# Heads' results scaled and split in PSUM, with every step of the plan given a new due time

## The chip, the cores and the metric

The kernel runs on one core of a Trainium2 chip. The metric is the device time of one execution in microseconds; smaller is better. TensorE (PE), VectorE (DVE), ScalarE (ACT) and GpSimd (POOL) each have an instruction stream of their own and meet through semaphores. SyncE (SP) issues all transfers.

## What is computed

Two blocks stand one after the other on x of shape (8, 1024, 512), in float32. The first is cross-attention with 8 heads of width 64; the second is self-attention with 16 heads of width 32, normalised queries, a gate over the heads' results, and a projection.

```python
def attn(q, k, v):                       # per head
    return softmax(q @ k.T * scale) @ v
# block X ("not ffn"), per batch
q = layernorm(x) @ Wq; k, v = ctx @ Wk, ctx @ Wv
x = x + tanh(g_xattn) * (heads(attn(q, k, v)) @ Wo + bo)
# block F ("ffn"), per batch
y = layernorm(x)
q, k, v = y @ Wq.T + bq, y @ Wk.T + bk, y @ Wv.T + bv
q = (q / norm(q) + query_embedding) * softplus(temperature)
h = heads(attn(q, k, v))
gates = softmax(h @ Wr.T + br); routed = top 3 of them; sw = softmax(h @ Ws.T + bs)
x = x + tanh(g_ffn) * ((h * sum of masked gates) @ Wp.T + bp)
```

## The kernel before

**Precision.** Every projection is made in three passes: a float32 operand is split into a rounded part ("hi", ScalarE, type fp32r) and the rest ("lo", VectorE, source minus hi), and hi·hi, hi·lo and lo·hi are summed in PSUM.

**Work and stages.** There are 16 batches of work: j = 0 to 7 are block X, j = 8 to 15 are block F. A batch has four groups g of 128 channels (2 heads of 64 in X, 4 heads of 32 in F), a group has two halves of 512 queries, and a half (number h, 8 in a batch) has 8 steps T of 128 keys. One step T is:

- `S` (PE, L1039): scores of 128 keys by 512 queries for each head e, on the whole array, into a PSUM bank;
- `ex` (ACT, L1237): the exponential, PSUM to SBUF (`probs`, `more`, `added`, `added_f`: a ring of 7 buffers in X, 10 in F);
- `ad` (POOL, L926): adds the exponentials of most steps to the half's running sum;
- `PV` (PE, L1053): probabilities times values, each head in its own columns of the array, summed over the 8 steps in one PSUM bank, called `acc`.

**The end of a half** is what the change rewrites. `sm` (PE, L1065) sums the exponentials, `sma` (ACT, L1244, L1245) takes the reciprocal into `rn`, `ev` (DVE, L1408, L1409, L1414) refines it and writes `h_raw = acc * rn` to SBUF, which empties `acc` and the bank of `sm`. Then `hs` (ACT, L1250) rounds `h_raw` to `h_hi`, in block F `gt` (PE, L1073) multiplies `h_raw` with the gates' weights, `hsl` (DVE, L1401) subtracts `h_hi` from `h_raw` in place, with both operands in SBUF, and `hw` (SP, L807) stores both parts. At the end of a batch `ol` (SP, L816) loads them back, `op` (PE) projects them, `ope` (DVE, L1465) adds to x, and `st` stores.

**Other work beside the steps**, which the text calls filler: `tr` (PE, L967) turns the normalised x, `pq`, `pk`, `vp` and `op` (PE, L947) are the projections, `mx` (PE, L1021, in row tiles) and `mxr` (DVE, L1378) find the scores' maxima, four PSUM banks at a time.

**The order.** All engines run one order that a planner (`Plan.run`) makes before compilation. It walks through time with a table of durations (`TAKES`). When an engine is free it takes, of the items whose predecessors are done, the one with the lowest due time, `step`, counted in steps T. The due time is the base in the code plus a per-kind offset from `AT[...]["off"]`. So due times decide between items that are ready and never make an engine wait. Items that write PSUM also need an empty bank of the eight; a bank is free once its taker is done. PE has one more term, quoted here: while PE is in a tiled mode (`PV`, `sm`, `mx`), untiled items are put back by `held` steps, and the other way round.

```python
wanted = lambda x: (step[x] + stage(batch(x)).AT["held"] * (name == "pe" and (x[0] in self.TILED) != (tiled is not None)), str(x))
...
elif it[0] in self.SHARED:
    begin = max(now, free["pool"])
```

The second quote is how the planner reckons with `hsl` and POOL: it delays `hsl` by what is left of POOL's present instruction.

## Time and profile before

| | us |
|---|---|
| median of 3 runs | 4856.84 |
| lowest, highest | 4849.66, 4885.29 |
| the profiled execution | 4888.63 |
| its span, first to last instruction | 4886.8 |
| PE busy | 4506.7 (92%) |
| POOL busy | 3385.7 (69%) |
| DVE busy | 3069.3 (63%) |
| ACT busy | 2523.6 (52%) |
| chain that ended last: share of PE | 76% |

All times in the profile are of one execution, which lies 32 us above the median of the timed ones. A matmul's end is modelled and consecutive matmuls overlap, so the cost of a matmul is read as the distance between starts, not as its duration. A number in square brackets at the end of a row of the timeline is the idle time just before it and what ended it.

### The profile page before, as it was taken

The numbers are of one execution on the slowest core, as the hardware profiler recorded it, in microseconds if no ns is written. First come the engines' busy times: TensorE is split into PE (matmuls) and PEld (weight loads), VectorE is DVE, ScalarE is ACT, GpSimd is POOL, SyncE is SP. The second block draws the span as 40 slices with busy tenths as digits, with TensorE's granted clock in tenths as the row PEclk, the third lists the DMA queues.
The fourth block names the chain that finished last, engine by engine and source line by source line (L and its number), as shares of the span: only waits on it lengthen the run. The fifth ranks groups of instructions, "written<-read, shape, count | busy, mean of one in ns | idle before, by whom it ended". The sixth has DMA issues, their size and how long they took to land.

```text
span 4886.8 us, 67578 instructions
## 1 busy us (share of the span) xinstructions
PE 4506.7 (92%) x21568; PEld 2325.8 (48%) x21568; DVE 3069.3 (63%) x3955; ACT 2523.6 (52%) x4577; POOL 3385.7 (69%) x2667
## 2 busy tenths in 40 slices
PE   4699999999999999999899899999998999989985
PEld 3355554555555555555354454544444544435432
DVE  4464646464646464676776767676767767676774
ACT  3253535353535353546556565656556556656562
POOL 1365666676757575667778778687877787877885
PEclk8899999999999999999999999999999999999997
DMA  6456656666666566545344344353534443543522
GB/s 221 111 160 177 177 168 179 179 180 186 160 175 166 159 169 164 157 138 151 91 127 134 83 132 134 89 154 104 139 100 118 130 134 84 145 121 89 154 70 78
DMA packets 516173, 682.50 MB, mean 140 GB/s; under 512 B 42608, under 2 KB 371824, under 8 KB 506608
## 3 DMA queue, kind: packets, MB, share of 16 engines
q1 hardware_dynamic: 515824, 678.18, 49.9%
q8 instruction: 178, 2.92, 0.3%
q14 instruction: 171, 1.40, 0.1%
HBM read 323.83 MB, written 150.99 MB: 97 GB/s over the span
## 4 chain that ended last, share of the span: by engine, by line
PE 76%; issue 7%; DVE 6%; ACT 4%; DMA 3%; POOL 1%; SPq 1%; ACTq 0%; POOLq 0%; DVEq 0%
PE aux L947 26%; PE aux L1039 19%; PE aux L1053 17%; PE aux L1021 7%; PE aux L1065 3%; DVE nm L1378 3%; ACT probs L1237 2%; DVE h_raw L1401 2%; SPq L836 1%; PE aux L991 1%; PE aux L1073 1%; POOL added_f L926 1%; PE aux L967 1%; ACT more L1237 1%; DMA raw<-in_ctxT 1%
## 5 line engine op out<-in xcount | busy, mean ns | idle before, releaser
L926 POOL TENSOR_TENSOR added<-added,probs 128x512 f32<-128x512 f32 x1433 | 1823.6, 1305 | 751.2 <-PE aux L1053 496.7
L1378 DVE TENSOR_REDUCE nm<-aux 128x2 f32<-128x1024 f32 x1536 | 1808.8, 1220 | 842.2 <-PE aux L1021 841.1
L1237 ACT ACTIVATE probs<-aux 128x512 f32<-128x512 f32 x2151 | 1190.9, 597 | 1141.8 <-PE aux L1039 1092.3
L1039 PE MATMUL aux<-stack 128*128 128x512 f32 x4096 | 1409.6, 437 | 103.8 <-ACT probs L1237 50.3
L1039 PEld LDWEIGHTS aux<-stack 128*128 128x128 f32 x4096 | 707.3, 191 | 950.0 <-issue 324.5
L1053 PE MATMUL aux<-probs,v 128*32 128x512 f32 (+1 forms) x4302 | 983.9, 628 | 0.0
L926 POOL TENSOR_TENSOR added_f<-added_f,probs 128x512 f32<-128x512 f32 x537 | 677.4, 1293 | 194.7 <-PE aux L1053 180.6
L947 PE MATMUL aux<-xT_hi,wqk 128*128 128x512 f32 x1536 | 562.0, 415 | 13.5 <-DVE mrow L1393 4.6
L1021 PE MATMUL aux<-ck_hi,cq_hi 32*128 32x512 f32 (+1 forms) x3072 | 460.1, 491 | 112.6 <-DVE nm L1378 90.8
L1021 PEld LDWEIGHTS aux<-ck_hi,cq_hi 32*128 32x128 f32 (+1 forms) x3072 | 182.1, 188 | 549.6 <-issue 529.5
L947 PE MATMUL aux<-wvo,parts 128*128 128x512 f32 x1536 | 409.0, 403 | 35.0 <-issue 35.0
L1237 ACT ACTIVATE more<-aux 128x512 f32<-128x512 f32 x537 | 300.6, 598 | 208.6 <-PE aux L1039 196.8
L947 PEld LDWEIGHTS aux<-xT_hi,wqk 128*128 128x128 f32 x1536 | 289.8, 189 | 136.6 <-issue 76.3
L947 PEld LDWEIGHTS aux<-wvo,parts 128*128 128x128 f32 x1536 | 279.7, 189 | 141.7 <-issue 87.3
L926 POOL TENSOR_TENSOR added_f<-added_f,more 128x512 f32<-128x512 f32 x231 | 295.0, 1301 | 46.1 <-PE aux L1053 42.8
L926 POOL TENSOR_TENSOR added<-added,more 128x512 f32<-128x512 f32 x231 | 293.3, 1295 | 36.1 <-ACT more L1237 21.7
L947 PE MATMUL aux<-xT_lo,wqk 128*128 128x512 f32 x768 | 301.9, 393 | 0.0
L1053 PE MATMUL aux<-more,v 128*32 128x512 f32 x1074 | 300.3, 634 | 0.2 <-ACT probs L1237 0.2
L1401 DVE TENSOR_TENSOR h_raw<-h_raw,h_hi 128x512 fp32r<-128x512 f32 x128 | 290.4, 2269 | 12.0 <-ACT h_hi L1250 12.0
L1053 PEld LDWEIGHTS aux<-probs,v 128*32 128x32 f32 (+1 forms) x4302 | 158.1, 120 | 277.0 <-issue 207.8
L914 POOL TENSOR_TENSOR cq_lo<-qb,cq_hi 128x512 fp32r<-128x512 f32 x64 | 82.7, 1292 | 200.9 <-ACT cq_hi L1196 200.9
L1237 ACT ACTIVATE added<-aux 128x512 f32<-128x512 f32 x256 | 140.6, 598 | 142.1 <-PE aux L1039 142.0
(129 smaller groups left out, 4355.6 us busy)
## 6 DMA issues: line engine op xcount, KB each, us to landing
wqk<-w_split SPq DMA_DIRECT2D x256, 256.0 KB, 3.7
wvo<-w_split SPq DMA_DIRECT2D x64, 1024.0 KB, 7.3
parts<-h_kept SPq DMA_DIRECT2D x128, 512.0 KB, 4.0
stack<-cq_hi SPq DMA_DIRECT2D x128, 256.0 KB, 5.7
stack<-ck_hi SPq DMA_DIRECT2D x128, 256.0 KB, 6.0
v_kept<-v_out SPq DMA_DIRECT2D x128, 256.0 KB, 2.7
v<-v_kept SPq DMA_DIRECT2D x64, 512.0 KB, 5.3
h_kept<-h_hi SPq DMA_DIRECT2D x128, 256.0 KB, 2.4
```

Of the source, the lines that this page charges most:

```text
L836: sp.dma_start(stack[row:row + D, g % 2, e * ph.SLOTS + slot, :].bitcast(F32), src[what][half][e * D:(e + 1) * D, :].bitcast(F32)).then_in ...
L914: pool.tensor_tensor(cq["lo"][:, q], qb[:, n], cq["hi"][:, q].bitcast(F32), ALU.subtract).then_inc(qlo_ok, 1)
L926: pool.tensor_tensor(onto, onto, exp_buffer(T, e), ALU.add).then_inc(added_ok, 1)
L947: ins = pe.matmul(out, lhs(a, k), rhs(c, k), start=k == 0 and i == 0, stop=k == whole - 1 and i == 2)
L967: ins = pe.transpose(out[:, i * P:(i + 1) * P], xs[:, i, k * P:(k + 1) * P], ident[:])
L1021: ins = pe.matmul(aux[:, b, :], cq["hi"][r, t * P:(t + 1) * P], ck["hi"][r, half * HALF:(half + 1) * HALF], start=True, stop=True)
L1039: ins = pe.matmul(out, stack[:, g % 2, e * ph.SLOTS + ks, jt * P:(jt + 1) * P], stack[:, g % 2, e * ph.SLOTS + qs, n * HALF:(n + 1) * HALF ...
L1053: ins = pe.matmul(out[e * D:(e + 1) * D, :], v[:, T // STEPS % 2, jt, e * D:(e + 1) * D], exp_buffer(T, e), start=jt == 0, stop=jt == TT - 1)
L1065: ins = pe.matmul(out[e * D:(e + 1) * D, :], ones[:, 0:ph.SUM], exp_buffer(T, e), start=i == 0, stop=i == ph.APART)
L1237: act.activation(exp_buffer(T, e), aux[:, o.bank["S", T, e], :], ACT.Exp, scale=ph.SCALE).then_inc(probs_ok, 1)
L1378: dve.tensor_reduce(nm[:, half, first:first + 2 * TT - t:TT], aux[:, b:b + 2, :], axis=AX.X, op=ALU.max, negate=True).then_inc(emptied["dv ...
L1401: dve.tensor_tensor(h_raw[:].bitcast(F32R), h_raw[:], h_hi[:].bitcast(F32), ALU.subtract).then_inc(h_lo_ok, 1)
```

## The change

In the diff `h_raw_ok` replaces `h_lo_ok`, and `h_lo` takes the place of the broadcast `bv` in SBUF.

1. `ev`'s last instruction multiplies `acc` by `rn` in PSUM, in place, and no longer waits for the store of the half before.
2. `hs` reads `acc` from PSUM. In F it adds the bias of the values, one number per channel.
3. New in F: `hr` (ACT) writes `h_raw` from `acc` plus bias, for `gt` alone. `gt` waits for it.
4. `hsl` reads `acc` from PSUM and `h_hi` from SBUF, and writes `h_lo` (F) or `h_raw` (X). It no longer waits for `gt`. The bank of `acc` is free only after `hsl`.
5. The bias of the values moves out of `vpe`: that becomes a plain copy.
6. `held` is 2.3 in X and 0.08 in F (it was 0), and nearly every kind of item gets a new offset.

```diff
-AT = (dict(p=[2.5, 15.14, 35.81, 48.12], over=7.63, held=0, mx0=-7.37, mxn=12.3, ctx=[18.4, 40.15, 13.68], load=[19.73, 48.58], norm=[28.97, 50.99], turned=[27.96, 23.9], vp=[38.13, 3], out=[1.5, 1.69], xr=-21.46, split=38.75, off={"ad": -0.59, "ln": 0.31, "pka": -0.33, "pkl": -1.14, "s2": 5.61, "gt": -1.09, "sma": -2.26, "trl": 2.36, "l2": 0.99, "mx": 0.07, "tra": 0.09, "mxr": -0.9}),
-      dict(p=[0.69, 18.6, 36, 50], over=6.09, held=0, mx0=-5.5, mxn=12.04, load=[51.51, 62.62], norm=[43.61, 30.7], turned=[30.5, 37.03], vp=[39, 3], out=[-1.13, 3.73], xr=-13.34, off={"trl": -0.94, "ad": -2.39, "tra": 1.65, "l2": 2.38, "cp": -4.87, "hsl": 0.44, "ev": -0.54, "ln": -0.9, "hs": -1.11, "sma": -1.35, "pqa": 1.36, "pkl": 0.75, "s3": 0.52, "pka": -0.28, "ssa": -0.53}))
+AT = (dict(p=[8.18, 7.74, 23.19, 56.95], over=13.88, held=2.3, mx0=-12.67, mxn=6.38, ctx=[9.31, 31.84, 65.87], load=[-19.58, 32.91], norm=[66.14, 26.24], turned=[17.66, 9.47], vp=[12.54, 5.88], out=[-4.13, 3.16], xr=-50.9, split=-100.42, off={"ad": 1.99, "ln": 5.75, "pka": -2.81, "pkl": 0.78, "s2": 5.61, "gt": -1.09, "sma": 8.55, "trl": 6.57, "l2": -7.13, "mx": -12.48, "tra": -4.24, "mxr": -2.4, "PV": 1.9, "S": 0.65, "ca": -11.36, "cd": -3.32, "ce": 8.23, "ci": -14.19, "cl": -2.55, "co": -2.71, "cx": 4.69, "cxl": -4.19, "cz": -2.4, "ev": 12.87, "ex": -11.45, "fb": -3.9, "fh": -12.84, "fi": 2.38, "fl": 2.62, "fr": 0.46, "fs": 3.83, "hs": 2.31, "hsl": -1.3, "hw": -1.65, "la": -14.63, "lb": 8.21, "mc": -5.82, "md": -26.04, "ml": -4.01, "mt": -3.87, "ol": 16.37, "op": -1.15, "ope": -1.02, "pk": -11.66, "pq": 1.59, "pqa": -4.8, "pql": 4.74, "sd": -1.5, "sm": 1.94, "st": 10.15, "tr": -9.24, "vl": 0.04, "vp": -10.27, "vpe": 3.66, "vs": 7.51, "wh": 7.3, "wl": 8.21, "wlo": -10.25, "wo": 3.99, "wr": -6.16, "ws": 9.98, "wv": 10.08, "xb": 2.46, "xl": -2.44, "xq": 6.09, "xr": 5.7}),
+      dict(p=[3.21, 20.36, 38.43, 52.49], over=5.98, held=0.08, mx0=-6.04, mxn=12.62, load=[100.75, -3.84], norm=[62.84, -8.24], turned=[-10.21, 12.16], vp=[40.89, 2.6], out=[5.06, 3.2], xr=-78.15, off={"trl": 0.44, "ad": -7.13, "tra": -1.33, "l2": 33.19, "cp": -4.87, "hsl": 3.98, "ev": 2.54, "ln": -11.36, "hs": 12.75, "sma": 10.04, "pqa": -2.45, "pkl": -8.4, "s3": -16.15, "pka": -11.02, "ssa": -16.48, "PV": -0.1, "S": -0.12, "ex": 0.85, "ga": -1.82, "ge": 5.92, "gm": -2.43, "gs": -1.15, "gt": -10.64, "hr": 7.79, "hw": -0.24, "la": 4.17, "lb": -6.25, "mc": 11.04, "md": 2.98, "ml": 28.19, "mt": -6.39, "mx": 1.12, "mxr": -5.35, "ol": -21.23, "op": 1.68, "ope": -17.26, "pk": 1.3, "pq": -1.15, "s2": 6.23, "s3p": -3.33, "sd": 2.14, "sm": -3.43, "ss": 0.5, "st": 1.37, "tr": -0.23, "vl": 0.77, "vp": -3.17, "vpe": -9.01, "vs": -0.29, "wl": 6.9, "wo": 0.81, "wv": -2.39, "xb": -1.89, "xl": 14.38, "xq": 1.37, "xr": -7.51}))
...
-                self.add(("ev", h), "dve", b + 0.6, [("sma", h), ("PV", T), ("ev", h - 1), ("hw", h - 1)])
+                self.add(("ev", h), "dve", b + 0.6, [("sma", h), ("PV", T), ("ev", h - 1)])
                 if ph.ffn:
-                    self.add(("gt", h), "pe", b + 1, [("ev", h), ("fb", 0)])
+                    self.add(("hr", h), "act", b + 0.9, [("ev", h), ("gt", h - 1)])
+                    self.add(("gt", h), "pe", b + 1, [("hr", h), ("fb", 0)])
...
-                self.add(("hs", h), "act", b + 1, [("ev", h)])
-                self.add(("hsl", h), "dve", b + 1.2, [("hs", h), ("gt", h)])
+                self.add(("hs", h), "act", b + 1, [("ev", h), ("hr", h), ("hw", h - 1)])
+                self.add(("hsl", h), "dve", b + 1.2, [("hs", h)])
...
-    SHARED = ("hsl", "fl")
+    SHARED = ("fl",)
...
-                        act.activation(h_hi[:], h_raw[:], ACT.Copy).then_inc(h_hi_ok, 1)
+                            act.activation(h_raw[:], src, ACT.Identity, bias=bias).then_inc(h_raw_ok, 1)
+                            continue
...
+                        if ffn:
+                            act.activation(h_hi[:], src, ACT.Identity, bias=bias).then_inc(h_hi_ok, 1)
+                        else:
+                            act.activation(h_hi[:], src, ACT.Copy).then_inc(h_hi_ok, 1)
...
-                        dve.tensor_tensor(v_out[:], src, bv[:], ALU.add).then_inc(emptied["dve"], 1)
+                        dve.tensor_copy(v_out[:], src).then_inc(emptied["dve"], 1)
...
                         dve.wait_ge(h_hi_ok, h + 1)
+                        whole = aux[:, o.bank["acc", h], :]
                         if ffn:
-
-                            wait_full(dve, ("gt", h))
-                        dve.tensor_tensor(h_raw[:].bitcast(F32R), h_raw[:], h_hi[:].bitcast(F32), ALU.subtract).then_inc(h_lo_ok, 1)
+                            ins = dve.scalar_tensor_tensor(h_lo[:], whole, bv[:, h // 2 % NG:h // 2 % NG + 1], h_hi[:].bitcast(F32), ALU.add, ALU.subtract)
+                        else:
+                            ins = dve.tensor_tensor(h_raw[:].bitcast(F32R), whole, h_hi[:].bitcast(F32), ALU.subtract)
+                        ins.then_inc(emptied["dve"], 1)
...
-                        dve.tensor_tensor(h_raw[:], aux[:, o.bank["acc", h], :], rn[:], ALU.mult).then_inc(emptied["dve"], 1)
+                        whole = aux[:, o.bank["acc", h], :]
+                        dve.tensor_tensor(whole, whole, rn[:], ALU.mult).then_inc(emptied["dve"], 1)
```

## Rows read from the trace of the kernel before

**Rows 1.** The page's busy times, share of the span, and instructions.

```profile
PE 4506.7 (92%) x21568; PEld 2325.8 (48%) x21568; DVE 3069.3 (63%) x3955; ACT 2523.6 (52%) x4577; POOL 3385.7 (69%) x2667
```

**Rows 2.** Windows (us; busy of PE, PEld, DVE, ACT, POOL; PEclk; DMA): one batch of X, one of F.

```profile
1165.00:1414.00 249.00, 248.45 (x1044) 132.28 (x1044) 132.83 (x178) 112.02 (x202) 160.22 (x123) 1.00 0.62 167
...
3621.00:3959.00 338.00, 311.18 (x1652) 156.26 (x1648) 242.98 (x313) 200.64 (x368) 261.11 (x208) 0.96 0.42 119
```

**Rows 3.** Timeline of PE (start, duration, what) in block X.

```profile
1302.49 1.20 PE L1039 MATMUL aux<-stack 128*128 128x512 f32 x4
1303.62 1.08 PE L1053 MATMUL aux<-probs,v 128*64 128x512 f32 x4
1304.63 0.28 PE L1027 MATMUL aux<-ident,least 128*16 128x128 f32 x1
...
1307.34 0.62 PE L947 MATMUL aux<-wvo,kv_hi 128*128 128x512 f32 x2
1307.80 0.39 PE L947 MATMUL aux<-wvo,kv_lo 128*128 128x512 f32 x1
```

**Rows 4.** Chain of work that ended last (start, length): two tiled runs in block F.

```profile
4700.67 0.99 PE aux L1053 x8
4701.67 1.72 PE aux L1065 x16
```

**Rows 5.** `hsl` before: ns min/median/max, first and last start; then busy us, mean ns.

```profile
L1401 DVE TENSOR_TENSOR h_raw<-h_raw,h_hi x128: 671/1185/35294, 183.8 to 4858.9; 128x512 fp32r<-128x512 f32 x128
...
L1401 DVE TENSOR_TENSOR h_raw<-h_raw,h_hi 128x512 fp32r<-128x512 f32 x128 | 290.4, 2269 | 12.0 <-ACT h_hi L1250 12.0
```

**Rows 6.** The same view of DVE instructions that read one operand from PSUM.

```profile
L1344 DVE TENSOR_TENSOR xT_lo<-aux,xT_hi x128: 669/681/694, 26.4 to 4421.6; 128x512 fp32r<-128x512 f32 x128
...
L1353 DVE SCALAR_TENSOR_TENSOR ck_lo<-aux,bk,ck_hi x64: 740/744/752, 2069.1 to 4672.7; 128x512 fp32r<-128x512 f32 x64
```

**Rows 7.** Timeline around one long `hsl`: DVE, PE, POOL.

```profile
2946.10 7.61 DVE L1401 TENSOR_TENSOR h_raw<-h_raw,h_hi 128x512 fp32r<-128x512 f32 x1
...
2955.11 0.78 PE L1021 MATMUL aux<-ck_hi,cq_hi 32*128 32x512 f32 x4 [4.45 <-DVE nm L1378]
...
2945.68 7.48 POOL L926 TENSOR_TENSOR added<-added,probs 128x512 f32<-128x512 f32 x6
```

**Rows 8.** The waits of PE in block F, 2250 to 4740 us (total, times, longest).

```profile
PE aux L1021 <- DVE nm L1378: 64.0, 23, 8.5
PE aux L1039 <- ACT probs L1237: 37.9, 103, 1.5
PE aux L1039 <- ACT more L1237: 19.5, 58, 1.5
PE aux L1039 <- DVE nm L1378: 18.1, 13, 9.3
```

**Rows 9.** Window just after the stall of rows 7 (columns as in rows 2).

```profile
2955.00:2960.00 5.00, 4.75 (x21) 1.95 (x22) 4.29 (x5) 1.57 (x3) 2.46 (x2) 0.66 0.79 225
```

**Rows 10.** The end: timeline of DVE and POOL, a window, and the chain.

```profile
4738.09 35.29 DVE L1401 TENSOR_TENSOR h_raw<-h_raw,h_hi 128x512 fp32r<-128x512 f32 x1
...
4806.73 25.12 DVE L1401 TENSOR_TENSOR h_raw<-h_raw,h_hi 128x512 fp32r<-128x512 f32 x1
...
4825.16 1.25 POOL L926 TENSOR_TENSOR added_f<-added_f,more 128x512 f32<-128x512 f32 x1
...
4760.00:4780.00 20.00, 7.31 (x42) 3.68 (x39) 15.90 (x6) 4.34 (x9) 12.83 (x11) 0.78 0.09 27
...
4815.46 22.88 issue
...
4851.43 1.90 PE aux L1065 x16
```

**Rows 11.** Start of block X: an idle time of PE.

```profile
196.81 1.22 PE L1021 MATMUL aux<-ck_hi,cq_hi 64*128 64x512 f32 x4 [9.31 <-DVE nm L1378]
```

**Rows 12.** Duration of ACT's read of a bank with a bias, as in rows 5.

```profile
L1162 ACT ACTIVATE ck_hi<-aux,bk x64: 668/672/712, 2065.9 to 4670.3; 128x512 fp32r<-128x512 f32 x64
```

## What I predicted, and why

> **What bounds the kernel now.** I read the page's busy times first, then windows by batch, then the timeline of PE, then the waits of PE, and last the chain at the end.
>
> PE is busy for 92% of the span, POOL for 69% [rows 1]. By batch the two blocks differ [rows 2]: a batch of X takes 249 us with PE busy throughout, a batch of F 338 us with PE idle for 27 us of it and a granted clock of 0.96. So X can be faster only if the same matmuls need less PE time. F can gain from its idle time too, and both blocks from their order.
>
> In X the time between starts shows what a matmul costs [rows 3]. Two passes of a projection take 0.46 us, 0.23 each. Four passes of `S` take 1.13 us, from 1302.49 to 1303.62, where four times 0.23 are 0.91: changing into the tiled mode and back costs 0.22. The four matmuls of a `PV` take 1.01 us. Where two tiled groups of the same mode follow each other, the second is cheaper: in F one `PV` takes 0.99 us, but the 16 matmuls of `sm` 1.72, that is 0.86 a group [rows 4]. So a `PV` that follows a `PV` saves 0.22 + 0.15 = 0.37 us. In the timeline of X from 150 to 2150 us there are 549 runs of column-tiled work with four matmuls, like that of [rows 3], and 13 longer ones. Nearly every `PV` pays in full.
>
> In F the waits of PE name `mxr`, the reduction of maxima on DVE, for 82 us, and the exponentials for another 57 [rows 8]. But `mxr` isn't slow: it is late, because `hsl` stood ahead of it on DVE. An `hsl` takes 671 ns at best, 1185 in the median and 35294 at worst [rows 5], 2269 in the mean, 290.4 us for all 128. The timeline shows what stretches it [rows 7]: one begins at 2946.10 and ends when POOL's unbroken run of six adds, begun at 2945.68, ends at 2953.16. PE idles 4.45 us for the maxima behind it. It does not happen to instructions that read one operand from PSUM: 128 and 64 of them, with POOL busy through much of their time, stay within 669 to 694 and 740 to 752 ns [rows 6].
>
> The Trainium skill, "SBUF — State Buffer", section "Who interferes with whom", states that a DVE instruction with two inputs in SBUF and a GpSimd instruction that reads SBUF exclude each other for the length of one instruction, and that one with at most one SBUF input doesn't contend. By that, an `hsl` would wait for one add at most, some 1.25 us, and the long stalls would not exist: the sum below would shrink to its terms for order. The trace agrees on who contends and disagrees on how long: 7.6 us are six adds [rows 7].
>
> **The change part by part.** The sum is made against the profiled span of 4886.8 us.
>
> *`hsl` reads PSUM.* Its nearest rows are those of [rows 6]: 0.68 us in X, 0.74 in F, always. DVE loses 290 - 64 x 0.68 - 64 x 0.74 = 199 us. What of it counts is where PE waited:
>
> - In F, 2250 to 4740 us, 13 idle times of PE lie behind an `hsl` of 7.6 to 11.9 us; that of [rows 7] is typical, they run from 1.3 to 9.3 us, together 65.6 of the 82 us of [rows 8]. All go: -65.6.
> - After such a stall the granted clock is 0.66 for 5 us though PE is busy again [rows 9]: 1.7 us lost each, 13 times: -22.
> - At the start of X the first `hsl`, begun at 183.8 us [rows 5], is followed by 9.3 us of idle PE, again for the maxima [rows 11]: -9.3. Later in X PE is busy throughout [rows 2], so nothing more is to be had from `hsl` there.
> - At the end two `hsl` take 35.3 and 25.1 us [rows 10]. The second holds back the store of half 62's result, hence the projection, and PE stands 22.9 us from 4815.5. The last sum `sm` begins at 4851.4. POOL sets the limit here: it worked without a pause except for 7.2 us in the window 4760 to 4780, and its last add ends at 4826.4. Without the stalls that would be 4819, and some 5 us of PE work fall between it and `sm`: 4824 in place of 4851, -27.
>
> *`ev` multiplies in PSUM, and doesn't wait for the store; `vpe` is a copy.* Same lengths (0.69 us) within a few hundredths. 0.
>
> *`hr` is new on ACT.* 64 instructions of 0.67 us [rows 12] are 43 us more on an engine that is busy 201 of 338 us in a batch of F. Behind each stand exponentials, for which `S` and PE wait. These waits are 57 us [rows 8] in some seven batches with 1400 us of ACT work [rows 2]; in proportion 43 us add 1.7. `gt` comes 0.7 us later, and nothing on PE waits for it but its bank. Bounds: 0, if always hidden, and 43, if each delays PE in full. I take +5.
>
> *`acc` keeps its bank until `hsl`.* Before, it was free after the multiplication; now ACT's copy or copies and `hsl` follow: 0.6 + 0.7 us in X, 2.1 in F if nothing else is in front. The due times put `hs` in F 12.75 steps back, so exponentials that are ready go first. The next half uses another bank, so what is missing is one bank of eight for `S` and filler. I charge nothing while it is a few us of the 40 of a half; a rival takes the rest.
>
> *`held` = 2.3 in X.* With `S` 0.65 and `PV` 1.9 later, the due times now put `S` about three steps ahead of `PV`, where the ring of 7 buffers ends, against two before; with `held` PE stays in a mode until the other side is over two steps overdue. So `PV` should come in pairs where the exponentials are ready. Of 560 runs in all of X, if half of the `PV` pair up, 140 changes go: 140 x 0.37 = -52. Bounds: 0 (pairing fails for lack of banks or exponentials) and 280 x 0.37 = -104 (all pair up).
>
> *All other due times.* In F the bases of projections and maxima stay near their old values and `held` is 0.08, so I expect the same pattern with the small waits for exponentials partly evened out. Besides `hsl`, F idles for 7 x 27 - 65.6 = 123 us [rows 2]. I take -15, an eighth of it, between -50 (two fifths evened out) and +30 (a quarter more of it). In the first 150 us x is now due before the weights, and one stall of the size of [rows 11] may come or go there, about 10 us either way. 0. Transfers are moved on SP's queue too (`xl`, `xr`, `ol`, the splitting of F's weights), past the stores of `hw`, `vs` and `st`. No transfer is among the waits of [rows 8], and in X PE doesn't wait at all [rows 2], so they have slack, and I give them no price.
>
> Sum: 4886.8 - 65.6 - 22 - 9.3 - 27 + 5 - 52 - 15 = 4700.9; with 1.8 us outside the span, 4703. The profiled execution is 32 us above the median of before. I don't carry that over: the long stalls depend on how DVE and POOL meet, so they may be what differs between executions, and the changed kernel wouldn't have them. If it is something else, 4671.
>
> **The rivals.**
>
> *A. The forecast*, 4703. Chance 0.48.
>
> *B. Stalls go, order gives nothing.* X is at 249 us a batch in any order if `PV` can't pair. Without the 52 and the 15: 4770. For it: `mx` takes four banks at a time and `acc` now holds its own longer, so that few are left to run `S` ahead. Chance 0.22.
>
> *C. The order gives all it can.* -104 in X and -50 in F: 4616. For it: F still idles 17 us a batch besides `hsl`. Against it: each exponential must still come before its `PV`. Chance 0.12.
>
> *D. Fillers in bunches.* In X `pk`, `vp`, `tr` and `mx` get due times some ten steps earlier, so they run as soon as they are ready, and stretches without filler follow. There POOL adds 7/8 x 2 x 1.25 = 2.19 us a step in X, against 1.13 + 1.01 = 2.14 on PE; in F 6/8 x 4 x 1.25 = 3.75 (an add takes 1.25 [rows 7]). In X bunching costs little, at most 0.05 x 512 = 26 us; in F a tenth of the steps without filler would cost 51 x (3.75 - 2.14) = 82, less half that the ring hides, 41. With it and without the gains of order: 4770 + 26 + 41 = 4837, within 1%. Chance 0.08.
>
> *E. The bank decides, and it is slower.* If `acc` is held for many steps because its `hs` stands behind exponentials, `S` runs with one bank fewer and PE waits for an exponential of 0.6 us at each step so affected. The other gains of A are 186 us, so it is slower than before from 186 / 0.6 = 310 of the 512 steps of F, five of a half's eight. In full it is 512 x 0.6 = 307 us: 4703 + 307 = 5010; with six of eight 4933. Against it: ACT is busy only 60% of a batch in F [rows 2], so `hs` finds room soon. The Trainium skill, "TensorEngine Tiling (Array Packing)", section "PSUM Bottleneck", warns that emptying PSUM may limit once matmuls are tiled; no row of before shows PE waiting for the bank of `acc`. Chance 0.07.
>
> *F. `hsl` still waits for POOL.* Then only the order counts: 4886.8 - 52 - 15 + 5 = 4825. The rows of [rows 6] speak against it. Chance 0.03.
>
> **How the numbers follow.** About 1% is what a measurement of this kernel can tell from no change. Faster by more: A, B, C and a quarter of D, 0.84. Within 1%, 4808 to 4905: the rest of D, and F, 0.09. Slower: E, 0.07. The range runs from C's 4616, less some of the 32 us, to above B: 4600 to 4795.
>
> **What would show it.** The subtraction of the rounded part never exceeds 0.8 us, and DVE's busy time falls by about 200 us. In F no idle time of PE above 3 us is put down to the maxima, and a batch takes 320 to 328 us. In X runs of eight column-tiled matmuls are frequent and a batch takes 240 to 245 us. The end has no idle time of 20 us. I am wrong if a batch of X still takes 249 us or more, or if PE's waits for exponentials in F grow by more than the stalls that go.

## The result, and the profile after

The changed kernel takes 4657.5 us (median of four, 4644.6 to 4669.8) where the kernel before, on the same chip, takes 4853.3 (4834.0 to 4885.3). The ratio is 0.959, with a 95% interval of 0.956 to 0.962: faster. The profiled execution took 4649.2 us, with a span of 4647.4.

The first table to make is by stage. The reciprocal `sma` starts once in each half, so its start in every eighth half marks a batch. All numbers are us, from one profiled execution of each kernel.

| | start to half 7 | X, six batches | X to F (halves 55 to 71) | F, six batches | last batch (119 to 127) |
|---|---|---|---|---|---|
| before | 407 | 1507 (251.1 each) | 608 | 2016 (336.0 each) | 316 |
| after | 379 | 1515 (252.5 each) | 577 | 1870 (311.7 each) | 273 |
| difference | -28 | +8 | -31 | -146 | -43 |

The table leaves out what follows half 127, 33 and 34 us. The profiled execution of before took 4888.6 us, 35 above the median of the four timed ones, and that of after lies 8 below its median. So the differences sum to 240 us where the medians differ by 196; up to 35 us of the row of before is not of the kernel but of that execution.

So nothing came from X, where 52 us were expected. F gave more than the forecast, and so did the start and the end.

The page's busy times, of the kernel after (those of before are [rows 1]):

```profile
PE 4358.8 (94%) x21568; PEld 2368.2 (51%) x21568; DVE 2883.9 (62%) x3955; ACT 2522.2 (54%) x4641; POOL 3339.1 (72%) x2667
```

DVE is busy for 185 us less. ACT has 64 instructions more and the same busy time. One batch of X and one of F, with columns as in [rows 2]:

```profile
1387.00:1642.00 255.00, 241.97 (x1046) 142.07 (x1044) 129.89 (x178) 108.74 (x202) 156.67 (x123) 0.97 0.60 163
3092.00:3404.00 312.00, 301.15 (x1656) 153.99 (x1653) 226.86 (x312) 203.83 (x377) 259.15 (x209) 1.00 0.46 129
```

Against [rows 2] both lines have changed their character. In F the idle time of PE fell from 27 us to 11, and the granted clock of TensorE rose from 0.96 to 1.00 of its full 2.4 GHz. In X PE is busy for 242 us instead of 248, so the matmuls did get cheaper, but it now stands idle for 13 us where it never stood before, and the clock is 0.97 instead of 1.00.

Durations in the kernel after, in ns min/median/max: `hsl` in F, `hsl` in X, and the new copy `hr`.

```profile
L1416 DVE SCALAR_TENSOR_TENSOR h_lo<-aux,bv,h_hi x64: 739/742/752, 2191.9 to 4618.1; 128x512 fp32r<-128x512 f32 x64
...
L1418 DVE TENSOR_TENSOR h_raw<-aux,h_hi x64: 679/692/694, 176.0 to 2152.4; 128x512 fp32r<-128x512 f32 x64
...
L1258 ACT ACTIVATE h_raw<-aux,bv x64: 679/701/757, 2189.1 to 4616.8; 128x512 f32<-128x512 f32 x64
```

The mean of 2269 ns [rows 5] is gone, and the longest of 128 is 0.752 us. The runs of PE in block X (start, duration, what) are longer than in [rows 3]:

```profile
1335.45 1.46 PE L1053 MATMUL aux<-probs,v 128*64 128x512 f32 x6
1336.84 2.15 PE L1039 MATMUL aux<-stack 128*128 128x512 f32 x8
1338.92 1.94 PE L1053 MATMUL aux<-probs,v 128*64 128x512 f32 x8
```

Counted by mode from 150 to 2150 us, there are now 86 runs of four column-tiled matmuls instead of 559, 111 runs of eight instead of two, and 63 still longer ones. Their total number fell from 562 to 260. (The 549 and 13 of the prediction are 559 and 3.)

The waits of PE (total, times, longest) in block F, 2250 to 4600 us, which answer to [rows 8]:

```profile
PE aux L1039 <- ACT probs L1237: 24.4, 59, 1.6
PE aux L1039 <- ACT more L1237: 10.5, 27, 1.2
...
PE aux L1021 <- DVE nm L1394: 4.8, 7, 0.8
```

The maxima cost 82 us before and the longest wait was 9.3; now no wait for them exceeds 1.0 us. And in block X, 250 to 2100 us:

```profile
PE aux L947 <- DVE aux L1430: 40.1, 7, 8.2
PE aux L947 <- issue: 27.9, 7, 4.8
PE aux L1039 <- ACT probs L1237: 17.3, 10, 4.1
```

The counts give them away: seven times each is once per batch. The first is new, and the second was 2.2 us in two waits before. Here is the first, in the timeline of DVE and PE (start, duration, what, and in brackets the idle time before and what ended it):

```profile
1475.85 2.48 DVE L1333 BATCH_NORM_STATS2 st<-xs 128x6 f32<-128x512 f32 x4 [9.02 <-DMA xs<-in_x]
...
1483.16 0.70 DVE L1430 TENSOR_TENSOR aux<-aux,rn 128x512 f32<-128x512 f32 x1
...
1484.00 0.77 PE L947 MATMUL aux<-kv_hi,wqk 128*128 128x512 f32 x1 [5.97 <-DVE aux L1430]
```

The layer norm of the next batch stands at the head of DVE's queue before its x has landed. The load was issued at 1464.97, among transfers for the stacks, and landed 10.85 us later. DVE stood for 9.0 us, and behind it stood `ev`, which PE needed.

The second is the output projection of a batch's last half. It waits for a store and a load of `h`, and these stood behind six transfers of a stack and a load of x (DVE's subtraction, SP's issues, then PE):

```profile
1390.90 0.69 DVE L1418 TENSOR_TENSOR h_raw<-aux,h_hi 128x512 fp32r<-128x512 f32 x1 [0.67 <-ACT h_hi L1266]
...
1396.59 1.09 SPq L807 DMA_DIRECT2D h_kept<-h_hi  x1
...
1403.68 0.33 SPq L816 DMA_DIRECT2D parts<-h_kept  x1
...
1407.79 4.58 PE L947 MATMUL aux<-wvo,parts 128*128 128x512 f32 x12 [3.33 <-issue]
```

The result was ready at 1391.6 and its store was issued at 1396.6. Each such stall costs twice, as in [rows 9]. These are windows of 5 us just after the two:

```profile
1408.00:1413.00 5.00, 5.00 (x16) 3.97 (x17) 0.59 (x1) 0.12 (x1) 0.00 (x0) 0.68 1.03 221
...
1485.00:1490.00 5.00, 5.00 (x14) 3.89 (x13) 2.07 (x3) 2.28 (x5) 2.52 (x2) 0.53 0.34 97
```

PE is busy throughout and starts 16 and 14 matmuls, where the next 5 us after the first stall, at a granted clock of 1.00, hold 24. So after an idle stretch of 3 to 6 us about 2 us more are lost. The granted clocks of 0.68 and 0.53 are means of stretches at 1.2 GHz and at 2.4 GHz.

### The profile page after: what moved, and what is told of

It reads as the page before. It is cut to its first block, busy times and chain, and to the rows that moved or that the text cites. A ratio compares the mean times of both kernels' runs of the same rounds, so it can differ in the third digit from the quotient of the medians.

```text
span 4647.4 us, 67798 instructions
## 1 busy us (share of the span) xinstructions
PE 4358.8 (94%) x21568; PEld 2368.2 (51%) x21568; DVE 2883.9 (62%) x3955; ACT 2522.2 (54%) x4641; POOL 3339.1 (72%) x2667
## 4 chain that ended last, share of the span: by engine, by line
PE 72%; issue 7%; DMA 6%; ACT 5%; DVE 4%; SPq 3%; POOL 2%; ACTq 0%; POOLq 0%; DVEq 0%
PE aux L947 29%; PE aux L1039 16%; PE aux L1053 15%; PE aux L1021 7%; PE aux L1065 3%; ACT probs L1237 2%; SPq L836 2%; DVE nm L1394 2%; DMA raw<-in_ctxT 2%; DMA xs<-in_x 2%; PE aux L991 1%; POOL added L926 1%; DMA xs<-x_after_xattn 1%; PE aux L1073 1%; PE aux L967 1%
## 5 line engine op out<-in xcount | busy, mean ns | idle before, releaser
L926 POOL TENSOR_TENSOR added<-added,probs 128x512 f32<-128x512 f32 x1433 | 1789.6, 1289 | 764.6 <-PE aux L1053 409.4
L1237 ACT ACTIVATE probs<-aux 128x512 f32<-128x512 f32 x2151 | 1171.9, 602 | 799.7 <-PE aux L1039 676.0
L1039 PE MATMUL aux<-stack 128*128 128x512 f32 x4096 | 1313.5, 427 | 97.3 <-ACT probs L1237 42.2
L1053 PE MATMUL aux<-probs,v 128*32 128x512 f32 (+1 forms) x4302 | 919.2, 609 | 1.6 <-ACT more L1237 1.1
L947 PE MATMUL aux<-xT_hi,wqk 128*128 128x512 f32 x1536 | 578.8, 413 | 7.6 <-ACT qb L1178 4.7
L947 PEld LDWEIGHTS aux<-wvo,parts 128*128 128x128 f32 x1536 | 292.7, 195 | 117.6 <-issue 57.0
L1053 PEld LDWEIGHTS aux<-probs,v 128*32 128x32 f32 (+1 forms) x4302 | 178.9, 120 | 328.3 <-issue 242.5
L926 POOL TENSOR_TENSOR added<-added,more 128x512 f32<-128x512 f32 x231 | 290.8, 1292 | 21.9 <-ACT probs L1237 15.8
L1053 PE MATMUL aux<-more,v 128*32 128x512 f32 x1074 | 283.9, 605 | 0.0
L1371 DVE TENSOR_TENSOR ck_lo<-aux,ck_hi 128x512 fp32r<-128x512 f32 x64 | 44.3, 692 | 263.3 <-ACT ck_hi L1164 263.3
L1426 DVE SCALAR_TENSOR_TENSOR aux<-aux,rn 128x512 f32<-128x512 f32 x128 | 88.9, 694 | 172.5 <-ACT rn L1245 171.9
```

The costliest lines, as they stand in the source:

```text
L926: pool.tensor_tensor(onto, onto, exp_buffer(T, e), ALU.add).then_inc(added_ok, 1)
L947: ins = pe.matmul(out, lhs(a, k), rhs(c, k), start=k == 0 and i == 0, stop=k == whole - 1 and i == 2)
L1039: ins = pe.matmul(out, stack[:, g % 2, e * ph.SLOTS + ks, jt * P:(jt + 1) * P], stack[:, g % 2, e * ph.SLOTS + qs, n * HALF:(n + 1) * HALF ...
L1053: ins = pe.matmul(out[e * D:(e + 1) * D, :], v[:, T // STEPS % 2, jt, e * D:(e + 1) * D], exp_buffer(T, e), start=jt == 0, stop=jt == TT - 1)
L1237: act.activation(exp_buffer(T, e), aux[:, o.bank["S", T, e], :], ACT.Exp, scale=ph.SCALE).then_inc(probs_ok, 1)
L1426: link(dve.scalar_tensor_tensor(src, src, -1.0, rn[:], ALU.mult, ALU.mult))
```

## The experiments

Twelve kernels ran, in three groups, each beside runs of the kernel before (medians 4852.2, 4852.3 and 4845.6 us). The changed kernel did not run again in these groups, so a difference from its 4657 us is uncertain by some 8 us, most of all for E10 to E13, the third group. In the diffs `...` marks what is left out, and a line of `AT` shows its first values only. "Batch" below is a batch's time from the marks of the table above. Five kernels, named at their place, have one more wait ahead of `sm`, for an exponential. In none of these does PE idle ahead of `sm` for exponentials for more than 3.7 us in the whole span, 0.3 us at a time.

### Body and due times apart

`e1_old_due` has the new body with all due times of before; `e2_old_body` has the body of before with all new due times (and the extra wait).

E1, against the changed kernel:

```diff
-AT = (dict(p=[8.18, 7.74, 23.19, 56.95], over=13.88, held=2.3,
+AT = (dict(p=[2.5, 15.14, 35.81, 48.12], over=7.63, held=0,
...
```

E2, against the kernel before:

```diff
-AT = (dict(p=[2.5, 15.14, 35.81, 48.12], over=7.63, held=0,
+AT = (dict(p=[8.18, 7.74, 23.19, 56.95], over=13.88, held=2.3,
...
+                        pe.wait_ge(probs_ok, ph.scores(end - 1, G - 1))
```

> The new body of a half's end with all due times of before. Theory 1 (the stalls behind the subtraction are what the body change is worth, 65.6 + 22 + 9.3 + 27 - 5 = 119 us): 4853 - 119 = 4734 us, a batch of F takes 336 - 13 = 323 us, a batch of X 249. Theory 2 (the due times do most of it): above 4800 us, a batch of F above 330 us.

> The body of before with all due times of the changed kernel (and one wait more ahead of the sum of the exponentials, on an exponential that is long done). Theory 1 (body and due times add up): the whole change is -196 us, the body -119, so the due times alone give -77: 4776 us, and subtractions of over 5 us still stand in F. Theory 2 (the due times do most of it): below 4720 us. Theory 3 (they need each other, since the new order puts the subtraction into longer runs of POOL): above 4820 us.

E1 took 4835.6 us, a ratio of 0.995 (0.993 to 0.997). E2 took 4919.6, a ratio of 1.014 (1.011 to 1.017). The body alone gives 17 us, the due times alone lose 67, and together they give 196. Neither is worth what it is worth beside the other. In E2 the subtraction is that of before and so are its stalls; in the new order they are longer, 350 us in all instead of 290 (the subtraction's durations, then one idle time of PE):

```profile
L1402 DVE TENSOR_TENSOR h_raw<-h_raw,h_hi x128: 680/1080/37886, 176.7 to 4885.3; 128x512 fp32r<-128x512 f32 x128
...
2877.37 0.80 PE L1021 MATMUL aux<-ck_hi,cq_hi 32*128 32x512 f32 x4 [12.93 <-DVE nm L1379]
```

A batch of F takes 344.7 us in E2. In E1 the stalls are gone, and yet a batch of F takes 331.2 us, only 4.8 less than before, and one of X 256.8, 5.7 more. So the body, with the order that the planner makes for it, has a cost of its own, which the later runs look for.

### What the lock of DVE and POOL is worth

`e4_sbuf_sub` keeps the changed kernel's order and gives F's `hsl` two operands in SBUF again. `e5_no_sub` keeps the order of before, and in the place of `hsl` has an instruction of the same length with one operand. In the traces PE and ACT run the same instructions in the same order in both pairs. E5 leaves out the subtraction of the rounded part. E4, against the changed kernel (`hr` then also waits until `hsl` of the half before has read its buffer):

```diff
-                            ins = dve.scalar_tensor_tensor(h_lo[:], whole, bv[:, h // 2 % NG:h // 2 % NG + 1], h_hi[:].bitcast(F32), ALU.add, ALU.subtract)
+                            ins = dve.tensor_tensor(h_lo[:], h_raw[:], h_hi[:].bitcast(F32), ALU.subtract)
```

E5, against the kernel before:

```diff
-                        dve.tensor_tensor(h_raw[:].bitcast(F32R), h_raw[:], h_hi[:].bitcast(F32), ALU.subtract).then_inc(h_lo_ok, 1)
+                        dve.tensor_reduce(aside[:], h_hi[:].bitcast(F32), axis=AX.X, op=ALU.max).then_inc(h_lo_ok, 1)
```

> The changed kernel in the same order, but in F the subtraction reads its first operand from the copy in SBUF that the gates use, so both operands are in SBUF, as before. Theory 1 (the long subtractions come from two operands in SBUF while POOL runs): single subtractions of over 5 us come back in F, and the time rises by 50 to 110 us, to 4710 to 4770. Rival (they came from the old order): none over 2 us, and the time stays within 15 us of 4657.

> The kernel before, in its own order, with one instruction changed on each of 128 halves: in place of the subtraction DVE reduces the rounded part from SBUF, one operand, about the same length. The low part of the heads' results is left out. Theory 1 (the stalls behind the subtraction are worth what the prediction said, 119 us with the +5 of the new copy left out, so 124): 4852 - 124 = 4728 us. Theory 2 (most of that time comes back at once, since PE then meets the next limit, POOL or the exponentials): above 4800 us, with a batch of F at 331 us as in the run with the new body and the old due times.

E4 took 4767.4 us, a ratio of 0.983 (0.979 to 0.986): 110 more than the changed kernel. The durations of its `hsl` in F, and the greatest of PE's waits from 2250 to 4740 us:

```profile
L1419 DVE TENSOR_TENSOR h_lo<-h_raw,h_hi x64: 681/1173/22203, 2193.8 to 4732.7; 128x512 fp32r<-128x512 f32 x64
...
PE aux L1039 <- DVE h_lo L1419: 77.4, 15, 9.8
```

E5 took 4738.5 us (4737.0 to 4740.4), a ratio of 0.977 (0.973 to 0.982): 114 less than the kernel before.

```profile
L1401 DVE TENSOR_REDUCE aside<-h_hi x128: 665/676/687, 183.6 to 4706.1; 128x1 f32<-128x512 f32 x128
```

Nothing else differs in E5, so this is the measured price of the lock, the mutual exclusion of DVE and POOL that stretches `hsl`. By stage, against the profiled execution of before (152 us apart, 35 of them its own excess), it is 13.2 us a batch in F, 39 in the last batch and 12 at the start. Of the 13.2, 9.1 are idle time of PE and 4.1 are busy time; from 2250 to 4740 us the waits for maxima fall from 82 us [rows 8] to 22 (total, times, longest):

```profile
PE aux L1021 <- DVE nm L1378: 12.1, 14, 2.4
...
PE aux L1039 <- DVE nm L1378: 10.1, 18, 0.9
```

E4 gives 110 and E5 114, each in its own order, both between medians. E5 also spreads over 3.4 us where the kernel before spreads over 39 in the same group, which fits long stalls that come out differently in each execution; the changed kernel, without them, still spreads over 25.

The record shows something more of the lock. Of the 128 `hsl` of before, 88 were stretched, and each of these ended 0.55 us after an instruction of POOL did. But 74 of them waited for one instruction only (two of these for a second one), and 64 of these although POOL went on behind it without a gap; the add that followed took 1.71 to 1.77 us instead of 1.25. One of them in the timeline of the kernel before, DVE and then POOL:

```profile
1524.65 1.26 DVE L1401 TENSOR_TENSOR h_raw<-h_raw,h_hi 128x512 fp32r<-128x512 f32 x1 [1.01 <-ACT h_hi L1250]
...
1522.84 9.16 POOL L926 TENSOR_TENSOR added<-added,probs 128x512 f32<-128x512 f32 x7
```

It ends at 1525.91, 6 us before POOL's seven adds do. Only 14 waited to the end of POOL's run, over 6 to 29 instructions, and behind 11 of them lie 63 us of PE's waits for maxima in F. In the kernel before and in E4 these 64 (40 in E4) short waits began when POOL had worked for at most 11 us without a gap, the long ones when it had for 24 us or more. In E2 one long wait began after 11 us and short ones after 15 and 17, so no fixed age of the run separates them. What does stays open.

### The bank of `acc`, held until `hsl`

E5 has neither the lock nor the held bank, E1 has no lock and holds it. `e9_no_sub_bank_held` is E5 with the bank freed by the instruction in `hsl`'s place, and leaves out the same part. Its order is planned anew, without the delay of `hsl` by POOL and without its wait for `gt`, so it isn't E5's: the order on PE differs from 183 us on. `e11_mixed` goes the other way: the changed kernel with all its due times, F's body new, and X's body as before, its bank free at `ev` (and the extra wait).

E9, against E5:

```diff
-                self.add(("hsl", h), "dve", b + 1.2, [("hs", h), ("gt", h)])
+                self.add(("hsl", h), "dve", b + 1.2, [("hs", h)])
...
-    SHARED = ("hsl", "fl")
+    SHARED = ("fl",)
...
-            return [(("ev", unit[1]), banks)]
+            return [(("hsl", unit[1]), banks)]
...
-                        dve.tensor_reduce(aside[:], h_hi[:].bitcast(F32), axis=AX.X, op=ALU.max).then_inc(h_lo_ok, 1)
+                        dve.tensor_reduce(aside[:], h_hi[:].bitcast(F32), axis=AX.X, op=ALU.max).then_inc(emptied["dve"], 1)
```

E11, against the changed kernel, the line that frees the bank:

```diff
-            return [(("hsl", unit[1]), banks)]
+            return [(("hsl" if stage(batch(unit)).ffn else "ev", unit[1]), banks)]
```

> The same, but the bank of acc is given free only after the place of the subtraction, as in the changed kernel, and the plan reckons with that. The low part is left out again. If the bank is what made a batch of X go from 251 to 257 us under the old due times: X at 256 to 258 us here, and 25 to 45 us more in the whole than the run without it; the rest of the way to 4836 us is the new copy of ACT in F. If the bank costs nothing: X at 251 us, and the same time within 8 us.

> X with the end of a half as before (acc's bank free after the multiplication, subtraction from SBUF), F with the new one, all due times of the changed kernel. If the bank of acc held longer is what X pays: a batch of X at 250 us or less instead of 252.5, F at 312, and the whole 15 to 25 us under 4657 us. If X's new order hides the bank: within 8 us of 4657 us. If F's order comes out differently behind another X: F at 320 us or more, as in the run with the old due times in X alone.

E9 took 4788.9 us, a ratio of 0.987 (0.982 to 0.992), 50 more than E5. A batch of X went from 249.9 to 256.7; one of F stayed, 322.8 and 322.6. One batch of X in E5, then in E9, columns as in [rows 2]:

```profile
1153.00:1402.00 249.00, 248.07 (x1044) 131.78 (x1042) 128.96 (x178) 112.33 (x201) 157.36 (x123) 1.00 0.61 167
```

```profile
1173.00:1429.00 256.00, 251.44 (x1044) 133.58 (x1040) 128.79 (x178) 111.55 (x201) 157.38 (x123) 0.99 0.59 162
```

The same 1044 matmuls; half of the 7 us is idle time, and half a longer busy time at 0.99. From the start of the reciprocal until the bank is free it takes 4.7 us in the mean in X in E5 and 7.1 in E9, in F 4.5 and 6.6. So 2.1 to 2.4 us more on one bank of eight, with the order planned for it, cost nothing in F and 6.8 us a batch in X. In X, from 400 to 1900 us, `S` waits longer for exponentials, whose reading frees a bank for it, in E9 than in E5, which fits a want of banks (E5, then E9; total, times, longest):

```profile
PE aux L1039 <- ACT probs L1237: 4.0, 6, 0.9
```

```profile
PE aux L1039 <- ACT probs L1237: 16.0, 8, 3.6
```

The rest of the new body costs X nothing: E1 has E9's order on PE up to 2296 us, and takes 256.8 us a batch against 256.7. But what the bank costs by itself and what the other order costs is not separated. E11, at 4714.4 us (ratio 0.972, 0.969 to 0.975), has a faster X under the new due times: 246.0 us a batch, 6.5 less than the changed kernel's. E2 has the same end of a half and the same due times in X as E11, with a plan that delays `hsl`, and takes 250.5, only 2.0 less. So the order alone moved X by 4.5 us a batch between these two, and neither 2.0 nor 6.5 is the bank by itself. That the held bank costs X something agrees with all of these runs; how much is open. That E11 isn't the faster kernel lies in F, where the planner, handed another state, made an order of 326.6 a batch from the same due times.

From E9 to E1 F still loses 8.6 us a batch. Three things differ, the copy `hr`, the longer chain of a half's result and the order that follows, and no run separates them.

### The copy `hr`

`e6_small_copy` is the changed kernel with `hr` on one column. It leaves out the rest of the gates' input.

```diff
-                            act.activation(h_raw[:], src, ACT.Identity, bias=bias).then_inc(h_raw_ok, 1)
+                            act.activation(h_raw[:, 0:1], src[:, 0:1], ACT.Identity, bias=bias).then_inc(h_raw_ok, 1)
```

> The changed kernel in its own order, the new copy of ACT in F (64 of 0.67 us) made on one column of 512 only, so that most of the gates' input is left out. If the copy costs what the prediction took: 5 us less, 4652 us. If each delays PE in full: 30 us less or more, under 4630 us.

4655.7 us (ratio 0.959, 0.954 to 0.965), a batch of F 312.3: 2 us of the whole, less than the runs differ among themselves. So the copy costs a few us at most, and 43 is ruled out.

### `held` in X

`e12_held0` is the changed kernel with `held` = 0 in X (and the extra wait).

```diff
-AT = (dict(p=[8.18, 7.74, 23.19, 56.95], over=13.88, held=2.3,
+AT = (dict(p=[8.18, 7.74, 23.19, 56.95], over=13.88, held=0,
...
```

> The changed kernel with held = 0 in X, all other due times kept. If the pairing is what keeps X from being slower with the bank held: runs of eight column-tiled matmuls become rare, PE is busy 247 to 250 us of a batch of X instead of 240, and X takes 257 us or more: 4657 + 35 or more. If the waits that came with the pairing cost as much as it gives: X stays at 250 to 254 us, with PE busy for all of it.

It took 4710.1 us (ratio 0.972, 0.969 to 0.975), 53 more than the changed kernel. A batch of X takes 259.1 instead of 252.5; from 150 to 2150 us 544 of 553 runs of column-tiled work have four matmuls again. One batch of X:

```profile
1417.00:1678.00 261.00, 253.13 (x1045) 133.79 (x1043) 130.12 (x178) 111.56 (x201) 156.39 (x123) 0.98 0.58 159
```

PE is busy for 253 us where the batch of the changed kernel shown above has 242. In the mean of six batches it is busy for 252.3 us and idle for 6.8 here, and 239.4 and 13.1 in the changed kernel. Pairing saves 12.9 us of PE's busy time a batch, and longer idle time takes back 6.3.

### Due times of X alone

`e3_old_x_due` gives X its old due times in the changed kernel (and the extra wait).

```diff
-AT = (dict(p=[8.18, 7.74, 23.19, 56.95], over=13.88, held=2.3,
+AT = (dict(p=[2.5, 15.14, 35.81, 48.12], over=7.63, held=0,
...
       dict(p=[3.21, 20.36, 38.43, 52.49], over=5.98, held=0.08,
...
```

> The changed kernel with the due times of before in X alone. If the pairing of tiled matmuls in X is worth its 8.7 us of PE time a batch and only new waits eat it up: a batch of X goes back from 253 to 249 us, the first batch loses the 28 us that the new start gave, and the whole comes to 4657 - 7 x 4 + 28 = 4657 us. If the new start is not owed to the due times of X: 4629 us.

4812.3 us (ratio 0.992, 0.990 to 0.995). X takes 257.5 a batch, as in E1. But F, with the same due times as the changed kernel, takes 327.2 instead of 311.7. So this is no measurement of X's due times alone: the planner carries its state from X into F.

### The stalls that are left in X

Three edits to the new stalls. `e8_ol_first` puts each batch's second load of the outputs behind the first. `e10_hw_first` moves the store of X's last half of a batch ahead of the stack's transfers. Both change only the order of SP's queue. `e13_xl_12` tells the planner that x lands after 12 us, not 9.7 (and the extra wait).

E8, the order in which SP's queue is made:

```diff
+                    if it[0] == "ol" and it[1] % TT == 0 and it[1] < TT * B:
+                        queue.append(("ol", it[1] + 1))
```

E10, the same place, for the store of a batch's last half (`late` is the place of the stack's transfers before it):

```diff
+                        queue.insert(late, it)
```

E13, the planner's landing times:

```diff
-... "xl": (1, 9.7), ...
+... "xl": (1, 12), ...
```

> The changed kernel with one edit in the order of SP's queue alone: in X the load of the second tile's parts (ol) stands right behind that of the first, ahead of the transfers of a group's stack. If PE's idle of some 4 us a batch before the second projected tile is owed to that place in the queue, it goes, and X is shorter by 8 x 4 = 32 us or a little less: 4625 to 4635 us. If another transfer or POOL is next at once: within 10 us of 4657 us.

> The changed kernel with one edit in SP's queue: in X the store of a batch's last half (hw) stands ahead of the stack's transfers (sd) instead of behind them, since the move of ol before it touched a load for which PE does not wait. The trace of the changed kernel has the subtraction done at 1391.5, the store issued at 1396.6 behind six stack transfers, the load at 1403.7 and PE's tile at 1407.8, after 3.3 us of idle. If the queue is the cause: the idle before the fifth projected tile falls from 3.3 to 5.4 us a batch to under 2, and the time by 10 to 25 us. If the stack's transfers then come too late: no gain, and a new wait of S.

> The changed kernel, planned with 12 us instead of 9.7 for the landing of the load of x (it took 10.8 in the trace, and VectorE stood 9 us at the head of its queue for it). If that wait is what stops PE for 3 to 8 us a batch before a projection of X: it goes, a batch of X takes 245 to 248 us, and the whole 35 to 55 us less than 4657. If the plan comes out differently and waits elsewhere: no gain, and the wait of VectorE for x gone all the same.

E8 took 4655.5 us, no change: a miss, since the projection waits for the part of the last half, and that load wasn't the one moved. E10 took 4643.3 (4639.9 to 4664.6), ratio 0.959 (0.955 to 0.963). The store is issued at 1390.5 instead of 1396.6 and its load at 1399.1 instead of 1403.7, and the idle time of the projections falls from 27.9 to 23.1 us. The place in the queue is a part of the cause, but a small one: 0.7 us of 4.0 a batch, where under 2 us of idle time were expected to stay. The ratio isn't to be told from the changed kernel's, and what makes the other 3.3 us wasn't tested.

E13 took 4696.2 us, ratio 0.969 (0.966 to 0.972). It does in X a part of what was expected. DVE's wait for x from 400 to 2000 us, in the changed kernel, then in E13 (total, times, longest):

```profile
DVE st L1333 <- DMA xs<-in_x: 54.0, 6, 11.2
```

```profile
DVE st L1334 <- DMA xs<-in_x: 23.4, 3, 9.6
```

X falls to 249.5 us a batch, where 245 to 248 were expected, and F rises from 311.7 to 318.6. Again the order of F pays, and the whole is slower than the changed kernel.

## Why the prediction was right or wrong

The forecast was 4703, in a range of 4600 to 4795; measured were 4657. The profiled executions differ by 239 us where the sum had 186. The total came close by luck: X gave nothing where 52 us were expected, the due times of F gave some 80 to 140 where 15 were, and the two errors had opposite signs. By the prediction's own sign ("a batch of X still takes 249 us or more") its account of X was wrong.

**The lock: right, in cause and size.** The steps for F, the start and the end sum to 124 us; E5 measured 114 at fixed order between medians, and 152 between profiled executions, against which the sum was made. In F the forecast was 88 us over some seven batches, about 12 each, and E5 has 13.2. At the start 9 were expected and 12 found. At the end 27 were expected; in the last batch, which also has its share of the 88, E5 gives 39 and the changed kernel 43. The last idle time of PE for a projection is now 6.6 us (the end's timeline), not 22.9 [rows 10]:

```profile
4626.36 7.39 PE L947 MATMUL aux<-wvo,parts 128*128 128x512 f32 x24 [6.56 <-issue]
```

The rule of the Trainium skill ("SBUF — State Buffer", "Who interferes with whom"), that whoever issues first holds the shared ports for the whole instruction, was read in the prediction as a wait of one add at most, and by that E5 would have gained little. It fits 74 of the 88 stretched `hsl` of before. For the other 14, behind which most of PE's waits for maxima lie, the measurement decides against that reading: DVE waited to the end of POOL's unbroken run. The statement of the Trainium skill in the same section that one operand in SBUF doesn't contend agrees with 128 `hsl` of the changed kernel, of 0.752 us at most.

**The clock after the stalls: right in the old order, but not all of the clock.** The 22 us were put down to the stalls of `hsl`. E5, without them and in the same order, is busy 4.1 us less a batch for the same matmuls (306.3 against 310.4), 29 over seven. But E1 has none of these stalls either, and its clock in F is still 0.97 (one batch, columns as in [rows 2]):

```profile
3533.00:3866.00 333.00, 313.76 (x1656) 157.75 (x1652) 226.43 (x312) 203.94 (x377) 258.47 (x208) 0.97 0.43 120
```

It has 19 us of other idle time of PE a batch. Over the kernels the two mostly go together: 0.95 at 35 us idle (E2), 0.98 to 0.99 at 17 (E5), 1.00 at 10 to 11 (the changed kernel, E12). E9, with 17 us and 0.99 to 1.00, shows that the amount of idle time alone doesn't set it.

**`hr`, +5: right as far as a run can tell.** 2 by E6, within its noise.

**The bank of `acc`, charged nothing: the step that failed.** The argument was that one bank of eight for a few us of 40 is free, and that if it cost anything it would be in F, where exponentials stand in front of `hs`. That was right for F (E9: 0) and wrong for X: 6.8 us a batch, 41 over the six, together with the order that the planner makes for the held bank. No row had shown X's need for banks, since PE was busy throughout; an engine that never waits shows no slack either. Of the whole kernel the held bank and its order are 50 us with the old due times. The warning of the Trainium skill that emptying PSUM may become the limit once matmuls are tiled ("TensorEngine Tiling (Array Packing)", "PSUM Bottleneck") fits X by E9, as far as later emptied banks made PE wait, and not F, where rival E had placed it. Rival E's form, one exponential of 0.6 us per step of F, was found in no run.

**`held` and pairing, -52: the net came out by luck.** E12 gives 6.6 us a batch, seven batches 46. But half of the `PV` were expected to pair up, and nearly all did: 260 runs instead of E12's 553, so that 293 x 0.37 = 108 us were to be had, the -104 of rival C. PE's busy time confirms it, 12.9 us less a batch, 103 over eight. The price of 0.37 was right; the share of pairs was half of what it became, and 6.3 us more idle time a batch, which the prediction had at nothing, took the difference away. The statement of the Trainium skill that changing the tiling mode drains TensorE ("TensorEngine Tiling (Array Packing)", "Key Properties") agrees with the busy time saved; that it is a drain no run shows.

So the forecast for a batch of X, 240 to 245 us, came out at 252.5. From the 251.1 of before, the held bank and its order add 6.8 (E9), the other new due times 2.4 (E12 against E9), and pairing with its stalls takes 6.6 away. The prediction said that transfers had slack, as none was among the waits of [rows 8]. This was the second fault: rows of the old order can't show the slack of a transfer that the new order issues elsewhere. Loads of x and the chain of the last half now cost PE 40.1 and 27.9 us over seven batches, and the clock after each. The second stands in E12 as well (29.2 us over six batches), the first doesn't.

**Due times in F, -15: too small by far.** A batch takes 311.7 us, against 331.2 with the same body in the old order (E1) and 322.8 in the order of before without the lock (E5): 11 to 19.5 a batch, so 80 to 140 us over seven batches, in place of 15. The bound of -50 was taken from F's idle time alone, 123 us, and from the guess that two fifths of it could be evened out. PE's idle time per batch fell from 19 (E1) to 11 us, which is close to that guess. The rest is busy time, 312.1 to 301.3 us for the same 1656 matmuls in the mean of six batches. In E1 PE is busy at the lower clock for 15.8 us of a batch, in the changed kernel for 0.6, and half of that difference, 7.6 us, is what the clock gives back; some 3 us are neither. So an eased order pays once in idle time and once more in clock, and only the first was counted. Why this order and not another gives it is only partly shown. The same due times of F gave 311.7, 313.0 (E12), 318.6 (E13), 326.6 (E11) and 327.2 (E3), depending on the state that X hands on; which of the placements makes the difference stays open.

**The start, 0: half seen.** -28 us, of which E1 (body) gives 12 and E2 (due times) 27, each alone.

## What to carry to other kernels

A DVE instruction with two operands in SBUF beside a POOL that works without pause can wait for many microseconds (14 of 128 did in the kernel before), and an operand left in PSUM removes it; but the bank it holds may have to be paid for where PE is saturated, so price it there and not where PE idles. When an order is planned anew, a change of the body and its due times must be judged together, since alone they gave 17 and -67 us of 196, and the rows of the old order bound neither the slack of transfers that move nor a gain that comes twice, in idle time and in the clock. A single due time can't be judged by the kernel's total: look by stage, because one block's gain is lost in the next.

## What the runs showed of the hardware

- The wait of DVE for POOL is mostly for one instruction of POOL (74 of 88 in the kernel before), but it can last to the end of POOL's unbroken run: 35.3 us before, 37.9 in E2, 22.2 in E4, for an instruction of 0.67 us. The median, 1.1 to 1.2 us, hides it. All 14 long ones of before began when POOL had run for 24 us or more without a gap.
- Column-tiled groups in 260 runs instead of 553 saved 12.9 us of PE's busy time in a batch of 1046 matmuls (the changed kernel against E12).
- One PSUM bank of eight, held for 2.1 to 2.4 us longer in each half and with the order planned for it, went with 0.85 us more a half where PE is busy all the time, and nothing where it idles for 5% of it (E9 against E5).
- After 3 to 6 us of idle time PE runs on at a granted clock of 0.53 to 0.68 over the next 5 us and starts 14 to 16 matmuls, where 5 us at 1.00 have 24 (windows of the changed kernel).
